# Pacing the second graph's gathers by TensorE's progress, in a two-layer graph network on one core

## The reference

```
# first graph: 200000 edges, sorted by destination
n  = layernorm(x)
x1 = x + relu(n @ W + segment_sum((n @ M)[src], dst))
# second block on n1 = layernorm(x1): 131072 edges plus self loops
h = n1 @ W_gat                       # 16 scores a node: 4 heads x 4 experts
e = leaky_relu(a_src[src2] + a_dst[dst2])
alpha = softmax of e over the edges of each destination
agg = segment_sum(h[src2] * alpha, dst2) + b_gat
w = weights of the best 2 of 4 experts, from layernorm(agg)
out = x1 + sum_e w[e] * (gelu(n1 @ W1[e] + b1[e]) @ W2[e] + b2[e])
```

## Time and profile before

| | us |
|---|---|
| runs of the kernel before | 4313.66, 4269.7, 4304.4 |
| their median | 4304.4 |
| span of the profiled execution, first to last instruction | 4291.8 |
| PE busy (13459 matmul instructions) | 2685.8 |
| PE weight loads | 2000.5 |
| DVE busy | 2156.3 |
| ACT busy | 902.7 |
| POOL busy | 2161.1 |

### The profile page before, as it was taken

One profiled execution on the slowest core, in us unless ns is written; L12 is line 12 of the kernel. 1 busy time (PEld: TensorE's weight loads), 2 busy tenths in 40 slices (PEclk: granted clock), 3 DMA queues, 4 the chain that ended last, 5 costly groups with the idle time before them and its releaser, 6 DMA issues. The chain is left out here.

```text
span 4291.8 us, 43359 instructions
## 1 busy us (share of the span) xinstructions
PE 2685.8 (63%) x13459; PEld 2000.5 (47%) x13459; DVE 2156.3 (50%) x5820; ACT 902.7 (21%) x1563; POOL 2161.1 (50%) x2248
## 2 busy tenths in 40 slices
PE   2465766676665676766777766761197555556754
PEld 1343544454443444554555544541196444445653
DVE  5676666666644444544444444420045444445666
ACT  3001111111122222111111111110054333334433
POOL 4565665556554565554555555557502434343121
PEclk9667988887887888888888888885598777777877
DMA  9575665655555565555555655540131111111146
GB/s 288 168 239 170 199 186 160 189 170 184 176 175 157 176 186 168 163 184 165 181 183 174 186 182 183 186 97 11 13 105 33 32 35 33 25 43 34 43 129 191
DMA packets 476804, 601.22 MB, mean 140 GB/s; under 512 B 72486, under 2 KB 415390, under 8 KB 474526
## 3 DMA queue, kind: packets, MB, share of 16 engines
q1 hardware_dynamic: 378766, 375.94, 26.7%
q0 software_dynamic: 97216, 219.88, 18.9%
q10 hardware_dynamic: 592, 2.64, 0.2%
HBM read 313.06 MB, written 286.79 MB: 140 GB/s over the span
## 5 line engine op out<-in xcount | busy, mean ns | idle before, releaser
L1700 POOL DMA_INDIRECT ring<-xn_d,srci x1611 | 1564.8, 971 | 1165.6 <-issue 453.7
L1504 PE MATMUL wide<-ring,one_hot 128*128 128x256 f32 x3222 | 984.0, 441 | 631.1 <-DVE ring L817 460.0
L817 DVE SCALAR_TENSOR_TENSOR ring<-ring,same_v,wide 128x256 f32<-128x256 f32 x1610 | 769.8, 478 | 1193.4 <-remote 662.5
L1504 PEld LDWEIGHTS wide<-ring,one_hot 128*128 128x128 f32 x3222 | 665.9, 218 | 900.3 <-issue 489.9
L1610 PE MATMUL wide<-tab_parts,low_hot 128*128 128x208 bf16 x6288 | 656.5, 261 | 334.1 <-issue 312.7
L1734 POOL DMA_INDIRECT g<-tab_d,srt x500 | 479.1, 958 | 633.3 <-DMA sum_d<-g 484.3
L1610 PEld LDWEIGHTS wide<-tab_parts,low_hot 128*128 128x128 bf16 x6288 | 575.6, 100 | 415.2 <-issue 380.3
L1562 PE MATMUL wide<-w2s,hh 128*128 128x256 f32 x1568 | 428.1, 422 | 149.6 <-issue 89.4
L1552 PE MATMUL wide<-xt,w1s 128*128 128x512 f32 (+1 forms) x832 | 423.4, 637 | 41.5 <-ACT hh L1237 39.4
L1237 ACT ACTIVATE hh<-wide,b1c 128x512 f32<-128x512 f32 (+1 forms) x208 | 137.7, 662 | 1469.0 <-remote 584.8
L1562 PEld LDWEIGHTS wide<-w2s,hh 128*128 128x128 f32 x1568 | 337.9, 217 | 225.7 <-issue 103.3
(11 more groups left out here) (369 smaller groups left out, 1740.9 us busy)
## 6 DMA issues: line engine op xcount, KB each, us to landing
run_d<-ring SPq DMA_DIRECT2D x201, 1024.0 KB
ring<-xn_d,srci POOLq DMA_INDIRECT x1611
y_d<-yo SPq DMA_DIRECT2D x196, 128.0 KB
comb<-y_d SPq DMA_DIRECT2D x28, 896.0 KB, 10.5
low_row<-low_d SPq DMA_DIRECT2D x13, 1024.0 KB
sum_d<-g SPq DMA_DIRECT2D x15, 768.0 KB, 3.4
g<-tab_d,srt POOLq DMA_INDIRECT x500
xn_d<-ring SPq DMA_DIRECT2D x7, 896.0 KB, 6.9
```

Of the source, the lines that this page charges most:

```text
L817: dve_at["run", j] = step(V.scalar_tensor_tensor(out=o, in0=ring[:, (j - 1) // JC % RING, (j - 1) % JC, :], scalar=same_v[:, j:j + 1], in1 ...
L1504: T.matmul(wide[:, 4 + j // 2 % 2, j % 2 * D:(j % 2 + 1) * D], one_hot[:, j // 4 % 4, j % 4, :], ring[:, j // JC % RING, j % JC, :], start ...
L1700: G.indirect_dma_start(out=ring[:, s, j % JC, :], out_offset=None, in_=xn_d, in_offset=at_rows(srci[:, j:j + 1])).then_inc(sem(f"gather{s} ...
```

## The change

Each gather of the second graph gets a wait ahead of it, or shares one with its neighbour. With `before_it` as the number of gathers ahead of it, the first 56 (`units_2`, as many as there are units in the second part) each wait until as many y units are done as stand before that unit in the list. The others wait, at each even number, for TensorE's block number (before_it - 56) / 4.4 + 1, rounded down. The wait for the slot (`sum_out`) stays, and so does the place of the scatters after chunk 0.

```
+PER_BLOCK = 4.4
...
+        units_2 = len(units) - units_1
+        ahead_of = [sum(what == "y" for what, _, _ in units[:units_1 + n]) for n in range(units_2)]
         for c in range(NCF):
             s = c % GR
             if c >= GR:
                 G.wait_ge(sem(f"sum_out{s}"), sent(c // GR - 1))
             for k in range(pool_cols[c]):
                 j = c * FC + k
+                before_it = sum(pool_cols[:c]) + k
+                if before_it >= units_2:
+                    if before_it % 2 == 0:
+                        G.wait_ge(sem("picked"), int((before_it - units_2) / PER_BLOCK) + 1)
+                elif ahead_of[before_it] > 0:
+                    G.wait_ge(sem("y_done"), ahead_of[before_it])
                 G.indirect_dma_start(out=g[:, s, k, :], out_offset=None, in_=tab_d,
                                      in_offset=at_rows(srt[:, j:j + 1])).then_inc(sem(f"feat_in{s}"), 16)
             if c == 0:
                 late_starts()
```

## The result

The changed kernel takes 4157.1 us (median of four runs, 4139.7 to 4166.7) against 4301.2 for the one before in the same comparison: a ratio of 0.967 (0.962 to 0.971), 144 us less. The forecast was 4230, 74 less than 4304.4. It is faster, as forecast, and inside the range, by about twice the forecast gain.

What follows compares the result with a forecast made beforehand. The prediction took TensorE to stand still behind POOL's runs of gathers, 1.4 us a request; -167 (units' stage) + 93 (paced blocks) + 0 + 0 = -74 us, from 4304.4 to 4230 us, range 4140 to 4315.

Steps and rivals of the forecast that it cites:

- Step (1): Units' stage: first 32 units run unstalled, then 48 requests drain; 122 us against 289, 167 us less.
- The lead: At TensorE: some 140 instructions already there, used up during gathers; lasts 7.1 us in blocks, 35.6 in the units' stage.
- Step (2): First 23.6 blocks: 104 gathers move there, two blocks' gathers merge, 8.3 us a block against 4.36; 93 us more.
- only drain-bound: Paced blocks: lower bound in which only the requests' drain sets the time, 6.1 us a block, 41 us more.
- Step (3): Gathers 160 to 499, chunks 5 to 15: POOL still waits for slots, eleven runs of 32 or 28 stay; 0 us.
- Step (4): Added waits, some 280 on POOL in all: under work that waits anyway, no deadline moves; 0 us.
- That every request costs the same however spaced: Rival, units' stage and blocks: 1.16 and 1.11 us lost per request, so nothing gained; 4304 us, 15%.
- That the lead doesn't refill: Rival, blocks 1 to 24: TensorE's instructions aren't replenished between runs, 12 us a block; 4336 us, 12%.
- That short runs don't hurt: Rival, paced blocks: pairs of gathers leave TensorE supplied, 0 to 41 us more there; 4137 to 4178 us, 20%.
- a forecast of no gain: Rival, whole change: TensorE's stops have another cause, as the skill's rule implies, so spacing moves nothing; 4304 us, 5%.

Runs made afterwards that it cites:

- g2_blocks_only: The changed kernel with the waits of the first 56 gathers removed, on a chip with stops: 0.975 of the kernel before.
- c3_seven_later: The changed kernel with the blocks' pace of 4.4 starting seven blocks later, on a chip with stops: 0.924 of the kernel before.
- c1: The kernel before, unchanged, run again on a chip with stops: 1.003 of the kernel before (4353.9 us).
- c2: The changed kernel, unchanged, run again on a chip with stops: 0.965 of the kernel before.
- g3_alone: A separate kernel with only matmuls beside gathers or plain DMAs in seven stages, on a chip with stops: 691.6 us, against 555.0 without stops.
- c4_pace_3_6: The changed kernel with 3.6 gathers a block in place of 4.4, on a chip with stops: 3934 us, 0.902 of the kernel before.

## Why the prediction was right in its sign and short in its size

**Step (1), the units' stage, has its size right**: 121.2 us where 122 was forecast. The paced 32 units run unstalled, and the requests behind them set the end; `g2_blocks_only` shows what is lost without the pacing (156). The way there is right only in part, and the near-exact figure is some luck. The lead was put at 35 us, so that all units would be done before TensorE stops and the first block stalls in their place; TensorE stopped after 64 matmuls, 19 us, with units still to do. So POOL did have gaps between gathers 31 and 55, 4.9 and 2.6 us, which the forecast named as not to be seen. The reading behind it was off: in the earlier trace rows the "same lead" is 113 matmuls, not the 69 and 71 of the earlier trace rows.

**Step (2), the size of a paced block, is one of the two terms that failed.** Forecast: 8.3 us a block and +93; measured +55.6 for the same 1410 matmuls, 6.7 us a block (4.36 + 55.6/23.6), 6.0 in the clean stretches. I let two blocks' gathers merge each time, with a stop and a stretch at the low clock behind each. In this stretch that happened three times. From a run of ten to the next gather it is 16.0 to 16.2 us, with 72 to 74 matmuls done, where the forecast had 16.6 us for 96: a merged piece costs more than I thought, but there are few. Elsewhere TensorE itself goes at the pace of the drain; as I read it, its block number then comes later, and so do the gathers that wait for it, which leaves the gap of 1.3 us on POOL. I had the value, 6.1 for "only drain-bound", as a bound, and took one above it by giving this feedback no part.

**Step (3), eleven volleys at 0 us, is the other.** The volleys stayed, each behind its slot, as forecast. But I took the block of a chunk's last gathers, 1.1 to 2.1 blocks after the slot's opening in the chunks of 32, as reached within the volley, by a lead of 1.5 blocks. It was reached only when TensorE was free again: in eight chunks the last 2 to 8 gathers come behind the recovery, which falls earlier by their number. In the three chunks of 28 the last block lies at most 0.6 after the slot's opening, and none comes apart. The eight cycles gain 45.8 us for 40 gathers, 1.1 us each. The bound given, 30 less, was itself too narrow. `c3_seven_later` shows the step's logic turned to use: with the pace behind all slots the volleys go altogether, and the blocks take 181 us less (1000.1 to 819.1).

**Step (4)**, no cost from the added waits, holds where there are stops, as far as it shows: the closing part moves 1.2 us. Without stops the waits cost up to 0.45%. (In the earlier trace rows POOL is busy four to seven tenths until near the end of its work, not a third to half; nothing hangs on it.)

-168 + 56 - 45 = -157 us in the stretches of the change, against -74 forecast; the chip's comparison gives -144, and c1 and c2, on one chip, -154.6 on the medians. Of the 83 us between -157 and -74, 37 are step (2) and 45 step (3).

**The rivals.** That every request costs the same however spaced falls: the same gathers leave TensorE 304 us idle for no visible cause in the blocks in one spacing and 63 in another, on one chip, and pairs alone cost none. That the lead doesn't refill falls too, at 6.0 us a block against the 10.6 from which it decides. That short runs don't hurt gave 4137 to 4178 and holds the measured time, but by luck: the paced blocks cost 56 us, more than its 0 to 41, since groups of four do slow a block, and the 45 us of the volleys, which it didn't have, make up for it. The Trainium skill's rule (Runtime: NRT & Kernel Launch, Instruction fetch mechanics), that fetching ahead is mostly hidden, fits the chips without stops, where the MOVE takes 29 to 38 ns and the change gains nothing. On the others the MOVE takes up to 1385 ns and a forecast of no gain misses it, whether or not instruction fetch is what stops TensorE.

**What stays open.** Why TensorE stops. The prediction took it for a shortage of instructions, whose DMAs hardly move beside gathers. For it speak the lead that is counted in matmuls (86 and 89 at 208 and 512 columns), SyncE's MOVE, and the idle time without a semaphore; the 64-column stage and the 113 and 64 matmuls of the units' stages fit only in part. Against it, as it was put, speak the instruction packets of `g3_alone`, which come after as many matmuls as elsewhere and as fast. What else the engines wait for no run shows; that the recording of the trace itself takes part wasn't tested either. Why chips differ isn't known; no run tells. The first part, with its 1611 gathers of `ring`, probably holds a larger loss of the same kind (it ends near 2850 to 2920 us on one kind of chip, near 2170 on the other); spacing wasn't tried there.

## What to carry to other kernels

Where TensorE's idle time is put down to nothing in step with POOL's indirect gathers, count the gathers and not their bytes, and let them follow the consumer's progress in twos to fours with a gap, at no more per block than the block's time over some 1.5 us (6.1 us for four in `c4_pace_3_6`). Set that pace behind whatever else releases the gathers (a buffer's slot), or they come in volleys all the same: on one chip pace 4.4 ahead of the slots gave 3.5%, the same pace behind them 7.6%, and 3.6 gave 9.8%. Before weighing parts against each other, see in the profile whether that chip has the effect at all; the best version here loses 0.3 to 0.45% on one that hasn't.

## What the runs showed of the hardware

- The same program takes 2997 to 3001 us on three chips and 4301 to 4354 on three others; the difference is in stops of TensorE, and of SyncE's MOVE with it, behind gathers that POOL issues. The granted clock goes with it, 0.93 over the whole kernel against 0.79 to 0.80 (0.81 for the changed one): it reads 0.54 to 0.62 over the stops of `g3_alone`, and 0.50, the 1.2 GHz level, in the first matmuls behind a stop.
- On a chip with stops 32 gathers in a row hold TensorE up until 45.0 us after the first, 1.41 us each, for rows of 96 bytes as for rows of 1 KB (43.5 and 45.1 us at 512 and 64 columns), though POOL issues one in 1.25 us.
- The lead is 86 to 89 matmuls of 208 and 512 columns, with about as many weight loads, where nothing else runs, and 69 to 71 in the blocks of the kernel.
- 32 plain DMAs of the same row size, issued by SyncE in 16.3 us, stop nothing, and neither do pairs of gathers 4.3 us apart.
- The instruction queue's packets of 16 KB, one for some 128 matmuls with their weight loads, come on a chip with stops after as many matmuls as on one without, one of them inside a stop.
